# Softplus' sum with the logarithm moved from VectorE to GpSimd, and two scatters moved behind a wait, in a fused Mamba and mixture-of-experts kernel

## The reference

```
x_ssm, x_gate = split(x @ in_proj_w.T + in_proj_b)
x_conv = silu(conv(x_ssm, 4 taps) + conv_b)
B, C   = split(x_conv @ bc_w.T + bc_b)              # 16 states each
dt     = softplus(x_conv @ dt_w.T + dt_b)
h_t    = h_(t-1) * exp(dt_t * A) + dt_t * B_t * x_t  # for 256 features x 16 states
y_t    = sum over states of h_t * C_t + x_t * D
z      = layernorm(layernorm_affine((y * silu(x_gate)) @ out_w.T + out_b + x) + x)
router: softmax over the 4 greatest of 8 logits of z
out    = layernorm(z + sum over the 4 experts of weight * swiglu_expert(z))
```

## Time and profile before

| what | value |
|---|---|
| median of 3 executions | 1278.99 us (1276.65 to 1279.28) |
| profiled execution, its own time | 1282.05 us |
| span of the profiled execution, first to last instruction | 1280.2 us |
| mean granted TensorE clock | 0.951 |
| busy: TensorE / VectorE / ScalarE / GpSimd | 1154.4 / 1042.5 / 872.6 / 740.7 us |

### The profile page before, as it was taken

How to read it: one execution, slowest core, us unless ns; L and a number is a source line. 1 busy time by engine, 2 the same in 40 slices (tenths; PEclk the granted TensorE clock), 3 DMA queues, 4 the chain that set the end, 5 groups by cost and what they waited for, 6 DMA issues and landing times. The chain is left out here.

```text
span 1280.2 us, 17873 instructions
## 1 busy us (share of the span) xinstructions
PE 1154.4 (90%) x5150; PEld 800.9 (63%) x5150; DVE 1042.5 (81%) x1796; ACT 872.6 (68%) x1553; POOL 740.7 (58%) x536
## 2 busy tenths in 40 slices
PE   8889998999999998686879999999999999999960
PEld 4334343535353534265768888888888888888850
DVE  4999999999999999975747777777777777777744
ACT  4676868686868695533747767777776777767744
POOL 0455759898989898966634344443344433444353
PEclk9889999999999998797989999999999999999985
DMA  2543536454555554544856666666665666666638
GB/s 104 220 166 132 197 118 213 171 210 174 201 183 191 194 190 154 196 174 163 272 162 167 168 158 150 142 167 168 157 152 141 168 166 157 158 139 164 166 42 270
DMA packets 69260, 217.23 MB, mean 170 GB/s; under 512 B 7520, under 2 KB 43232, under 8 KB 56288
## 3 DMA queue, kind: packets, MB, share of 16 engines
q1 hardware_dynamic: 33888, 171.63, 38.3%
q0 software_dynamic: 26880, 36.72, 17.0%
q10 hardware_dynamic: 8448, 8.39, 2.0%
HBM read 165.55 MB, written 51.15 MB: 169 GB/s over the span
## 5 line engine op out<-in xcount | busy, mean ns | idle before, releaser
L1118 DVE TENSOR_TENSOR_SCAN state<-decay,p_bu 128x512 f32<-128x512 f32 x256 | 297.0, 1200 | 0.0
L662 PE MATMUL p_y<-read,small 128*128 128x512 f32 x512 | 255.3, 639 | 37.0 <-POOL read L1312 36.9
L1637 POOL DMA_INDIRECT total<-o_v,tok x144 | 251.8, 1749 | 39.6 <-issue 39.2
L662 PEld LDWEIGHTS p_y<-read,small 128*128 128x128 f32 x512 | 101.1, 203 | 176.4 <-issue 111.9
L1635 POOL TENSOR_TENSOR scrap<-neg_half 128x1 f32<-128x1 f32 x36 | 23.2, 644 | 320.0 <-ACT o_v L1549 317.5
L520 DVE TENSOR_SCALAR up_v<-up_v 128x512 f32<-128x512 f32 x144 | 68.4, 475 | 148.7 <-ACT up_v L515 146.1
L512 ACT ACTIVATE gate_v<-p_g,bias 128x512 f32<-128x512 f32 x144 | 98.6, 685 | 125.7 <-PE p_up L502 124.7
L862 ACT ACTIVATE decay<-dt,scan_rate 128x511 f32<-128x511 f32 x256 | 162.2, 710 | 8.7 <-DVE state L1118 8.6
L1354 POOL DMA_INDIRECT queues<-rows,index x128 | 131.2, 1025 | 32.8 <-issue 30.9
L1312 POOL TENSOR_TENSOR read<-state,bc 128x1024 f32<-128x1024 f32 x64 | 127.6, 2000 | 27.8 <-DVE p_bu L1109 13.5
L533 ACT ACTIVATE ah<-a_v 128x512 fp32r<-128x512 f32 x144 | 91.3, 634 | 57.3 <-DVE a_v L526 57.3
(11 more groups left out here) (236 smaller groups left out, 2955.7 us busy)
## 6 DMA issues: line engine op xcount, KB each, us to landing
bc<-bc_rows SPq DMA_DIRECT2D x32, 1024.0 KB, 5.5
first_raw<-in_w_experts SPq DMA_DIRECT2D x19, 1668.0 KB
raw_w<-in_w_experts SPq DMA_DIRECT2D x18, 1668.0 KB
first_wh<-bc_rows SPq DMA_DIRECT2D x16, 1024.0 KB
first_wl<-bc_rows SPq DMA_DIRECT2D x16, 1024.0 KB
first_rows<-queues SPq DMA_DIRECT2D x19, 544.0 KB
xq<-queues SPq DMA_DIRECT2D x18, 544.0 KB
queues<-pad SPq DMA_DIRECT2D x9, 544.0 KB
```

The source lines that it names most:

```text
L662: mm = pe.matmul(p_y[h][:, :], ident[:, :], read[:, t % 4, h, :], start=False, stop=(t == SLOTS - 1))
L1118: dve.tensor_tensor_scan(state[t % 4][:, h, :], decay[(SLOTS * s.n + t) % AHEAD][:, h, :], p_bu[:, h * LEN:(h + 1) * LEN], 0.0, ALU.mult, ...
L1637: pool.indirect_dma_start(total, bass.IndirectOffsetOnAxis(ap=tok[t.p][:, a:a + 1], axis=0), o_v[t.p][:, a, :], None, compute_op=ALU.add). ...
```

## The change

GpSimd makes the sum with the logarithm in the rounds 0 to 6, in slot 10 right behind its own part of the softplus, and ahead of its product 10. It adds `logp` to `rest` where VectorE added it to `relu`; VectorE's `scan_inputs` (dt = relu + rest) stays as it is, and waits for the same two semaphores. The scatters 4 and 5 leave slot 12 for the place of scatter 6, in slot 15 behind the wait for p_u and product 14, in the rounds 2 to 6. In round 7 the scatters have a table of their own, which is not changed.

```diff
@@ VectorE, dve_stage1
                 if r.like == Round.FIRST and t == 10:
                     softplus_rest(r)
                     add_log(r)
-                if r.a and r.b and t == 13:
-                    add_log(r)
                 if r.a and t == 13:
                     scan_inputs(r)
@@ GpSimd, pool_stage1
+        def add_log(r):
+
+            s = r.s.at(1)
+            pool.wait_ge(s_log, s.n + 1)
+            pool.wait_ge(s_rest, s.n + 1)
+            pool.tensor_tensor(rest[:, :, :], rest[:, :, :], logp[:, :, :], ALU.add).then_inc(s_sum, 1)
+
@@
-        SCATTERS = {8: (0, 1, 2), 10: (3,), 12: (4, 5)}
-        BEHIND_DRIVE = (6,)
+        SCATTERS = {8: (0, 1, 2), 10: (3,)}
+        BEHIND_DRIVE = (4, 5, 6)
         NEXT_TO_LAST = {8: (0, 1, 2), 10: (3,), 11: (4, 5), 12: (6,)}
@@
                 if r.a and r.b and t == 10:
                     softplus_rest(r)
+                    add_log(r)
                 if r.d and r.a and t == SLOTS - 1:
                     scatter(r.s.at(-2), BEHIND_DRIVE)
```

## The result

| | kernel before | changed kernel |
|---|---|---|
| median | 1279.05 us (1276.65 to 1279.28, 4 runs) | 1306.60 us (1296.48 to 1308.31, 4 runs) |
| ratio | | 1.0203, interval 1.015 to 1.0257 |
| profiled execution | 1282.05 us, span 1280.2 | 1308.31 us, span 1306.5 |

The change makes the kernel some 2% slower. Forecast were 1298.9 us and a range from 1285 to 1305; the direction came as forecast, the median lies 1.6 us outside the range. The single times of the changed kernel are not one cluster: 1296.48, and 1306.03 to 1308.31.

A forecast was written before the change was run, and what follows sets the result against it. VectorE was taken to bound the scan stage, busy 64.34 of 64.68 us; 13.2 + 6.4 + 0.25 = 19.9 us over 1282.05 gave 1301.9, less 3.06 for the median: 1298.9 us, range 1285 to 1305.

The forecast's parts named there:

- (1): VectorE, rounds 0 to 6: loses seven additions with a mean of 1.21 us, 8.5 us in all.
- (2): GpSimd, slot 10: the addition takes 2.36 us, ends 2.43 us after the logarithm; VectorE waits 1.5 us, spending the saving.
- (3): dt's sum on VectorE: kept out by product 10, ends 5.47 us after the logarithm in every round; +13.2 us.
- who is first: At dt's sum: product 10 begins ahead of VectorE, by 0.08 us; the term is 3.04 us, 1.26 if VectorE is first.
- the remainder: At dt's sum: VectorE's sum ends 1.09 us after product 10, as p_u did after GpSimd's products.
- The rule that I set against it: At dt's sum: instructions exclude each other for their whole length, so the full 1.23 us follows product 10; 1.0 us more.
- (4): Slot 15: two more scatters delay product 15 by 2.37 us, TensorE and logarithm by 1.6, rounds 3 to 6; +6.4 us, bounds 0 and 9.5.
- A: Rival: no exclusion at dt's sum, TensorE late all the same; +7.7 us, 1286.7 us; chance 0.18.
- B: Rival: exclusion at dt's sum, but the late product 15 is absorbed; +13.2 us, 1292.2 us; chance 0.12.
- C: Rival: neither exclusion at dt's sum nor a late TensorE; +1.0 us, 1280.0 us; chance 0.06.
- D: Rival: faster, GpSimd's sum is there before VectorE reaches slot 13; 8.5 us saved, 1270.5 us; chance 0.08.
- E: Rival: the norm's small operations go ahead of dt's sum too; up to 9.6 us on top, 1308.5 us; chance 0.06.

The follow-up runs named there:

- the transposes: Changed kernel with the router's transposes made three times over in rounds 3 to 7, same result in the same bank: 1295.86 us, ratio 1.0143.
- the second profile of the changed kernel: Changed kernel run once more with nothing altered: median 1301.14 us, ratio 1.0203; the profile is of its first execution, 1296.36 us.
- the version that beats both: Kernel before, in rounds 0 and 1 alone GpSimd adds relu to rest, VectorE then adds logp, waits moved in round 1: 1273.94 us, ratio 0.9976.
- the sum behind product 10: Changed kernel with GpSimd's addition of the logarithm behind product 10 instead of ahead of it: median 1296.59 us, ratio 1.0177.

## Why the prediction was right, and where it failed

**(1) and (2), the saving and GpSimd's addition: right.** 2.35 us against 2.36, 0.07 or 0.08 us behind the logarithm, and the seven additions gone from VectorE without a gain.

**(3) dt's sum behind product 10: right.** 5.46 or 5.47 us behind the logarithm in all seven rounds, forecast 5.47. The step that rested on 0.08 us, who is first, held in all six rounds in which VectorE stood waiting (in round 0 product 10 had begun 1.2 us before VectorE came), and the remainder was 1.08 as p_u's rows had shown. The rule that I set against it (the Trainium skill, SBUF — State Buffer, section Who interferes with whom) would have had the full 1.23 behind product 10; the measurement decides for 1.08. One gain was missed: in the kernel before p_u took 2.49 us in round 2; after the change it takes 1.44 there, 1.05 us less, and in round 1 it ends 0.3 us earlier behind dt.

**(4) The late product 15: the first part right, the bound wrong.** p_u to product 15 was 5.92 us (forecast 5.9), TensorE's wait 2.93 (2.9), the logarithm 54.44 us behind p_u where the clock held, 1.6 more than before. Up to dt's end of round 6 the steps gave 19.6 us, and the execution whose clock held in the rounds 3 to 6 shows 487.21 - 467.98 = 19.2. That this is so near is luck in part: 1.4 us of gains at p_u that I missed and an earlier first logarithm stand against 1.4 us more in round 1. With the transposes, and round 1 as before, it was 18.6. The failed step is the sentence that bounds this term by "4 x 2.37 = 9.5": it takes TensorE's speed behind a longer wait from rows at a granted clock of 1.00, which were read behind a wait of 0.51 us. With a wait of 2.93 it fell to 0.50 in rounds 3 and 6, and partly in 4: 5.0 + 1.45 + 0 + 5.0 = 11.5 us in the profiled execution, by which the term was 17.9 and not 6.4. I had asked what the wait costs TensorE, not what it does to the pace of the work behind it, though that work was the one full stretch of the round. With the clock as a term, 0 to 12 us more, the range would have reached to about 1310.

VectorE's wait for the sum was forecast at 3 us from round 3 on; it was 1.73 to 2.04. VectorE had lost time before it, by the waits listed above in the rounds with a lower clock, and otherwise by 0.24 at lg and by one small operation of the router's that met a product. This is round 5 of the second profile of the changed kernel, with GpSimd's product at 385.65; before, the same row took 0.18 us:

```profile
386.57 1.16 DVE L1210 TENSOR_TENSOR ex<-ex,chosen 128x32 f32<-128x32 f32 x1
```

The time was not touched by it, since dt's sum followed the logarithm and not VectorE. Two readings of mine were loose: the norm's small operations are three (L1322, L1324, L1326) and not four, and the 0.07 us for the signal was taken from no row; the runs then showed 0.07 to 0.08.

The rivals: A (no exclusion), B (the late product absorbed), C and D (faster) are excluded by the distances above; in E dt's sum is kept out by more than one operation, which showed in no run; that E's price, 1308.5 us, lies near the median is chance.

The change in the profiled spans, 26.3 us, is less than the 30.0 up to round 6. The profiled execution of the kernel before spent 705.4 us from the last lg to the end, the twelve others 698.1 to 700.5, one of them of a kernel without the change (the version that beats both). Why is open.

## What to carry to other kernels

Moving 1.2 us of work off the engine that bounds a stage gains nothing if the new owner has to wait for the same input, and an addition that is followed at once by another operation of GpSimd can keep VectorE's consumer of that sum out for the length of that operation: put the work that needs no late operand ahead, as relu here, and what has to be quiet behind a wait. Where a second engine is full up to the next hand-over, price any longer wait ahead of that stretch at both levels of its clock. And before a stage's scatters are moved, look for the product that they then stand in front of.

## What the runs showed of the hardware

- After a wait of 2.93 us of TensorE for product 15, which followed one of 2.5 us for product 11 and in some rounds one of 1.2 for product 14, the granted clock fell to 0.50 in some rounds and stayed at 1.00 in others of the same program. In the first profile it stayed down for some 10 us in the rounds 3 and 6 and for less than 5 in round 4. With the wait cut to 1.18 us by matmuls of no use it did not fall at that place in any of the rounds 3 to 6. (It falls about slot 13 too in most rounds, before the change as after it: before, behind a wait of 2.66 us for product 11, it was 0.50 from 342.5 to 345 us. TensorE then has waits for GpSimd ahead of it.)
- In these rows a VectorE operation with two SBUF operands and a GpSimd operation on SBUF are exclusive both ways, and the one that waits is next: p_u behind product 12 ahead of product 13, dt's sum between two operations of 0.2 and 1.0 us. VectorE's operation ends 1.08 or 1.09 us after GpSimd's, less than its 1.23 alone. A small one is held as well: 1.16 us in place of 0.18.
- How much shorter than 2.93 us the wait has to be for the clock to hold, and what decides between the rounds of one execution, is open; one wait of 1.94 us (round 5 with the sum behind product 10) went by without a fall.
